# Metaformer block on one core: values stored with zeros between a pair's heads, one gated product and one output matmul a tile

## The chip, the cores and the metric

The kernel runs on one core of one Trainium2 chip, in float32. The metric is the device time of one execution, in microseconds; the median of several runs is compared.

## The reference

The input x is (16, 64, 64, 64): n images, rows a, columns b, 64 channels. Four sublayers follow one another, each added to x; this change touches the first alone, attention over the image axis.

```
zn  = layernorm(z) * ln_w + ln_b                 # over the 64 channels
q,k,v = zn@Wq, zn@Wk, zn@Wv                      # 8 heads of 16 channels
g   = sigmoid(zn @ Wg + bg)
att = softmax over j of q[i,a,b,h,:] . k[j,a,b,h,:] / 4      # i, j: the 16 images
out = (sum_j att[i,j] * v[j]) * g, reshaped @ Wo + bo
```

Then: a router picks 2 of 8 experts (softmax, top 2, renormalized) per token; an exponential moving average over the rows a gates a linear expansion; last, an expert-choice layer for each image (32 experts, 8 tokens each), which is the kernel's second stage.

## The kernel before

**Steps.** The first stage holds the first three sublayers. Its unit is half a column b: 4 tiles (QT) of 128 tokens, a token block being 8 rows a by 16 images. 64 columns of two halves give 128 steps. In the code a step is `step(i, q)`, column i, half q; q = 0 is called an even step here, q = 1 an odd one. The stages of a half are spread over successive steps by the table `LAG` (projections lag 1, scores 2, values and output 3, experts 4, expansion 5, moving average's output 7), so that within one step every engine works on several halves. Each engine has its own program, written out by hand in a fixed order, the same in every step; semaphores alone tie them (`filled[...]`, `drained[...]`, `s_og`, ...). Only even steps hold the moving average: its scan on VectorE (L926) and its tanh `ema_t` on ScalarE (L564). The gating product `gated` (L800) is computed at the end of the even step for one half, and in the midst of the odd step for the other.

**Attention in a step.** TensorE transposes a normalized half; ScalarE copies it to `zT`. Four projections follow: q, values (L670), gate, k (L608 and L609, the last into `s_bank`). ScalarE makes eight masked copies of the keys, `kT`, one a head (L472), spread over its program (heads 0 to 1, 2 to 3, 4 to 5, 6, and 7 as the last of the step). A step later L640 multiplies them with the queries: 32 tokens at a time, two accumulating products each, to give the scores in `s_bank`. VectorE takes the maximum and subtracts it, ScalarE takes exp, VectorE sums and inverts, with `own_den` (L857) made so that each head of a pair gets its denominator or zero. GpSimd multiplies these out into `probs` (L414), which holds for every pair of heads two blocks, one with the first head's probabilities and zeros, one with the second's; VectorE transposes (L918).

**The values.** ScalarE copies the values out of PSUM into `v_sb` (L504); GpSimd adds their bias (L406). L658 multiplies, for each tile t, each pair of heads k and each group g of 32 tokens, the 32 x 32 block of `v_sb` (both heads of the pair) with 64 moving columns of `probsT`. The result `o_bank` has 64 columns a tile and group, 32 for each head of a pair, and in either only one head's rows are meant. VectorE multiplies both halves with the gate `gT` into `ogT` (L839, twice), and L687 multiplies them with the output weights, two accumulating matmuls a tile: `w_o2[:, 0]` keeps the first heads' rows, `w_o2[:, 1]` the second heads' (the factor 0.5 of the sigmoid is in them). The gate is tanh of half its argument (ScalarE, `gT`, L512), plus one (ScalarE, L561, late in the step); the sigmoid is half of that.

**Who waits for whom around it.** `gT` is written when its last reader `ogT` is done (`s_og`). L640 waits for the last key copy (`drained["k"]`). The x1 sum (L868 on VectorE) waits for L687. The router's chain follows on VectorE up to `lgm` (L888), and ScalarE's `lge` (L541) waits for that; the last four key copies stand behind `lge` on ScalarE.

A float32 matmul appears in the trace as two matmul records and two weight loads.

## Time and profile before

| | |
|---|---|
| three timed runs | 3136.28 us median, 3127.79 to 3141.26 |
| profiled execution | its span is 3121.5 us; no other time of it is given |
| TensorE matmul, weight loads | busy 2647.5 us (85%), 1969.9 us (63%) |
| VectorE | busy 2551.6 us (82%) |
| ScalarE | busy 2005.1 us (64%) |
| GpSimd | busy 2161.0 us (69%) |
| mean granted TensorE clock | 0.839 of full |
| L658 value products | 16384 records, 196.5 us |
| L687 output products | 2048 records, 246.9 us |
| L406 add of the values' bias | 128 of 1274 ns on GpSimd |
| L839 `ogT` | 256 of 679 ns on VectorE |

The span is from the first to the last instruction. A busy share is a mean over all stages; the first stage takes nearly all of the span. Matmul records overlap, so the busy time of a group is the time in which at least one of them ran.

### The profile page before, as it was taken

What the parts mean: (1) busy time and instruction counts of PE and PEld (TensorE: products, weight loads), DVE (VectorE), ACT (ScalarE), POOL (GpSimd) and SP (SyncE); (2) the same over time, 40 slices, a digit from 0 to 9 for tenths busy, and PEclk for the clock granted to TensorE, in tenths of its full rate; (3) what the DMA queues carried; (4) which work ended last, traced back from release to release, by engine and by line L of the source; (5) the groups of instructions that cost most, each with busy time, mean ns of one, the idle gap of its engine ahead of it and who ended that gap; (6) DMA issues with size and microseconds to landing.
All of it is one profiled execution on the core that took longest, in us unless ns stands there. A gap on an engine that the chain in (4) does not pass through costs nothing. (4 is left out here: it accounts for less than half of the span.)

```text
span 3121.5 us, 108500 instructions
## 1 busy us (share of the span) xinstructions
PE 2647.5 (85%) x37071; PEld 1969.9 (63%) x37071; DVE 2551.6 (82%) x9002; ACT 2005.1 (64%) x3590; POOL 2161.0 (69%) x2963
## 2 busy tenths in 40 slices
PE   2898898888888888898898898888988988896697
PEld 2666666666666656666666666666666666664586
DVE  2788889888888898888888888888889888885604
ACT  2666767766676676776776766677667676762600
POOL 2677777877777777777787877778777777863000
PEclk9788988887888888888887987889889788885858
DMA  0011101111011010110101111011010010101828
GB/s 17 9 20 18 19 17 19 19 18 19 17 19 18 18 19 17 19 19 18 19 17 18 19 18 19 17 19 19 18 19 18 17 19 18 19 15 19 269 96 337
DMA packets 263153, 106.67 MB, mean 34 GB/s; under 512 B 250257, under 2 KB 254900, under 8 KB 258997
## 3 DMA queue, kind: packets, MB, share of 16 engines
q1 hardware_dynamic: 260933, 93.16, 12.9%
q10 hardware_dynamic: 2160, 12.68, 1.0%
q8 instruction: 40, 0.66, 0.1%
q14 instruction: 20, 0.16, 0.0%
HBM read 55.31 MB, written 50.33 MB: 34 GB/s over the span
## 5 line engine op out<-in xcount | busy, mean ns | idle before, releaser
L472 ACT ACTIVATE kT<-s_bank,b_k,block_of 128x512 f32<-128x512 f32 x1024 | 748.8, 771 | 3.6 <-PE s_bank L609 0.3
L640 PE MATMUL s_bank<-kT,qT 128*32 128x128 f32 x8192 | 396.1, 372 | 187.3 <-issue 187.3
L640 PEld LDWEIGHTS s_bank<-kT,qT 128*32 128x32 f32 x8192 | 349.5, 152 | 226.8 <-issue 224.7
L489 ACT ACTIVATE qT<-shared,b_qkg 128x256 f32<-128x256 f32 x256 | 107.5, 471 | 412.0 <-PE shared L609 412.0
L811 DVE TENSOR_REDUCE mixed<-yg 128x256 f32<-128x2048 f32 x128 | 288.5, 2254 | 0.2
L687 PEld LDWEIGHTS o_bank<-w_o,ogT 128*128 128x128 f32 x2048 | 247.9, 193 | 23.7 <-DVE ogT L839 14.8
L414 POOL TENSOR_TENSOR probs<-weights,own_den 128x1024 f32<-128x1024 f32 x128 | 252.7, 1975 | 1.8 <-DVE own_den L857 1.8
L687 PE MATMUL o_bank<-w_o,ogT 128*128 128x64 f32 x2048 | 246.9, 274 | 4.3 <-DVE ogT L839 3.9
L387 POOL TENSOR_TENSOR split_ffn<-norm_ffn,split_ffn 128x256 fp32r<-128x256 f32 x128 | 93.6, 731 | 215.1 <-ACT split_ffn L464 215.1
L658 PEld LDWEIGHTS o_bank<-probsT,v_sb 32*32 32x32 f32 x16384 | 170.2, 107 | 63.7 <-issue 58.1
L658 PE MATMUL o_bank<-probsT,v_sb 32*32 32x64 f32 x16384 | 196.5, 234 | 1.5 <-DVE yg L932 1.5
L387 POOL TENSOR_TENSOR split_att<-norm_att,split_att 128x256 fp32r<-128x256 f32 x128 | 94.0, 735 | 147.4 <-ACT split_att L464 147.4
L622 PE MATMUL shared<-bias,ones 3*128 3x512 bf16 x256 | 109.3, 427 | 98.3 <-ACT picks L532 52.2
L555 ACT ACTIVATE gpre<-shared,bgate_col 64x256 f32<-64x256 f32 x256 | 181.4, 709 | 13.3 <-PE shared L721 10.3
L593 PE MATMUL shared<-ident,split_att 128*128 128x128 f32 x512 | 111.6, 357 | 69.3 <-ACT prim L555 47.9
L377 POOL TENSOR_TENSOR rstd_ffn<-rstd_ffn,minus_half 128x4 f32<-128x4 f32 x128 | 160.1, 1251 | 10.7
L406 POOL TENSOR_TENSOR v_sb<-v_sb,bv_rows 128x512 f32<-128x512 f32 x128 | 163.1, 1274 | 3.0 <-ACT v_sb L504 3.0
L839 DVE TENSOR_TENSOR ogT<-o_bank,gT 128x512 f32<-128x512 f32 x256 | 163.2, 679 | 1.5 <-PE o_bank L658 1.2
L918 DVE STREAM_TRANSPOSE probsT<-probs 128x1024 f32<-128x1024 f32 x128 | 157.9, 1234 | 2.0 <-POOL probs L414 2.0
L593 PEld LDWEIGHTS shared<-ident,split_att 128*128 128x128 f32 x512 | 78.4, 182 | 123.3 <-issue 68.2
L800 DVE SCALAR_TENSOR_TENSOR gated<-ema_t,prim 64x256 f32<-64x256 f32 x256 | 150.3, 587 | 6.8 <-ACT ema_t L564 1.1
L677 PE MATMUL shared<-w_con,gated 128*128 128x64 f32 x1024 | 141.8, 283 | 7.9 <-DVE gated L800 5.8
(204 smaller groups left out, 7648.6 us busy)
## 6 DMA issues: line engine op xcount, KB each, us to landing
x_in<-in_x SPq DMA_DIRECT2D x1024, 16.0 KB, 1.7
x_scratch<-x SPq DMA_DIRECT2D x1024, 16.0 KB, 1.4
normalized_x_scratch<-norm_pick SPq DMA_DIRECT2D x1024, 16.0 KB, 1.5
xa<-normalized_x_scratch SPq DMA_DIRECT2D x16, 1024.0 KB, 8.1
xb<-x_scratch ACTq DMA_DIRECT2D x8, 1024.0 KB, 10.3
out_x<-xa SPq DMA_DIRECT2D x16, 512.0 KB, 5.3
out_x<-xb SPq DMA_DIRECT2D x16, 512.0 KB, 6.9
xa<-x_scratch SPq DMA_DIRECT2D x4, 1024.0 KB, 6.5
```

The source lines that it names most:

```text
L377: ch.link(g.tensor_tensor(r[:, 1, :], r[:, 0, :], minus_half[:], ALU.pow))
L387: g.tensor_tensor(split[kind][z][:, :, 1, :], norm[kind][z][:], split[kind][z][:, :, 0, :].bitcast(F32), ALU.subtract).then_inc(s_split[ki ...
L406: g.tensor_tensor(v_sb[z][:], v_sb[z][:], bv_rows[:].unsqueeze(1).broadcast_to([P, QT, HC]), ALU.add).then_inc(s_v, 1)
L414: g.tensor_tensor(probs[:], weights[:].unsqueeze(2).broadcast_to([P, 32, 2, 16]), own_den[:].unsqueeze(3).broadcast_to([P, 32, 2, 16]), AL ...
L472: ins = s.activation(kT[:, h, :], bk("k")[:], ACT.Identity, bias=b_k[:, h:h + 1], scale=block_of[:, h:h + 1])
L555: ins = s.activation(dst, src, ACT.Identity, bias=bias[r0:r0 + D], scale=scale)
L593: ins = t_.transpose(bank_of(q, name)[:, t * P:(t + 1) * P], split[kind][par(q, lag)][:, t].rearrange("p k d -> p (k d)").bitcast(F32), id ...
L640: ins = t_.matmul(s_bank[g * 32:(g + 1) * 32, 0, t * P:(t + 1) * P], qT[z][:, c, tok:tok + 32], kT[:, :, tok + c * N:tok + (c + 1) * N], s ...
L658: ins = t_.matmul(o_bank[k * 32:(k + 1) * 32, g, t * 64:(t + 1) * 64], v_sb[z][g * 32:(g + 1) * 32, t, k * 32:(k + 1) * 32], pT[g * 32:(g ...
L687: ins = t_.matmul(bk("att_out")[:, t * D:(t + 1) * D], ogT[:, h, tile(t)], w_o2[:, h, :], start=(h == 0), stop=(h == 1))
L811: v.tensor_reduce(mixed[:], yg[:], AX.X, ALU.add).then_inc(s_mixed, 1)
L839: ins = v.tensor_tensor(by_group(ogT[:, h, :]), o, by_group(gT[z][:]), ALU.mult)
```

## The change

The values are stored with zeros between the heads of a pair: `v_sb` has, for each tile and pair, three slots of 16 channels, and only the outer two are written; the middle one is set to zero once, ahead of the steps. A 32-wide window over slots 0 and 1 is the first head with zeros, one over slots 1 and 2 zeros with the second head. L658 becomes two products for each tile, pair and group, one a head, each with 32 moving columns, added up in PSUM. So `o_bank` has 32 columns a tile and group, all of them meant, and `ogT` becomes one scalar_tensor_tensor: (product + values' bias, now a column) times gate. The output takes one matmul a tile. Since the bias is added there, GpSimd's add to `v_sb` is gone; in its place in GpSimd's program stands gate plus one, and ScalarE's is gone. `zT` and `gT` are written with the order of 32-token blocks exchanged, so that `ogT` reads and writes straight runs. The bias column comes from a fourth matmul of the setup.

```diff
@@ weights and buffers
-            w_o2 = cb("w_o2", [P, 2, D])
+            w_o2 = cb("w_o2", [P, D])
-            bv_rows = cb("bv_rows", [P, HC])
+            bv_col = cb("bv_col", [P, 1])
-            v_sb = cpair("v_sb", [P, QT, HC])
+            v_sb = cpair("v_sb", [P, QT * 4, 3, C])
-            ogT = cb("ogT", [P, 2, QTOK])
+            ogT = cb("ogT", [P, QTOK])
@@ GpSimd
-                        pool.wait_ge(drained["v"], at(i, q, 1))
-                        g.tensor_tensor(v_sb[z][:], v_sb[z][:], bv_rows[:].unsqueeze(1).broadcast_to([P, QT, HC]),
-                                        ALU.add).then_inc(s_v, 1)
+                        wait_apart(pool, (drained["gate"], at(i, q, 1)))
+                        g.tensor_scalar(gT[z][:], gT[z][:], 1.0, None, ALU.add).then_inc(s_gp1, 1)
@@ ScalarE
-                        s.copy(zT[z1][:], bk("att_t")[:]).then_inc(drained["att_t"], 1)
+                        s.copy(zT[z1][:].rearrange("p (g t i) -> p t g i", g=4, t=QT),
+                               bk("att_t")[:].rearrange("p (t g i) -> p t g i", g=4, t=QT)).then_inc(drained["att_t"], 1)
-                        s.copy(v_sb[z1][:].rearrange("p t c -> p (t c)"), bk("v")[:]).then_inc(drained["v"], 1)
+                        s.copy(v_sb[z1][:, :, 0:3:2, :], bk("v")[:].rearrange("p (k m c) -> p k m c", m=2, c=C)).then_inc(drained["v"], 1)
-                        s.activation(gT[z1][:], bk("gate")[:], ACT.Tanh, bias=bg_col[:],
+                        s.activation(gT[z1][:].rearrange("p (g t i) -> p t g i", g=4, t=QT),
+                                     bk("gate")[:].rearrange("p (t g i) -> p t g i", g=4, t=QT), ACT.Tanh, bias=bg_col[:],
-                        act.wait_ge(drained["gate"], at(i, q, 1))
-                        s.activation(gT[z1][:], gT[z1][:], ACT.Identity, bias=one_col[:]).then_inc(s_gp1, 1)
@@ TensorE
-                        wait_apart(pe, (s_probsT, at(i, q, 3)), (s_v, at(i, q, 3)), (s_og, at(i, q, 4)),
+                        wait_apart(pe, (s_probsT, at(i, q, 3)), (drained["v"], at(i, q, 3)), (s_og, at(i, q, 4)),
-                                for g in range(4):
-                                    ins = t_.matmul(o_bank[k * 32:(k + 1) * 32, g, t * 64:(t + 1) * 64],
-                                                    v_sb[z][g * 32:(g + 1) * 32, t, k * 32:(k + 1) * 32],
-                                                    pT[g * 32:(g + 1) * 32, t, 2 * k:2 * k + 2, :],
-                                                    tile_position=(g * 32, k * 32))
+                                for h in range(2):
+                                    for g in range(4):
+                                        rows = slice(g * 32, (g + 1) * 32)
+                                        ins = t_.matmul(o_bank[k * 32:(k + 1) * 32, g, t * 32:(t + 1) * 32],
+                                                        v_sb[z][rows, t * 4 + k, h:h + 2, :].rearrange("p m c -> p (m c)"),
+                                                        pT[rows, t, 2 * k + h, :], start=(h == 0), stop=(h == 1),
+                                                        tile_position=(g * 32, k * 32))
-                            for h in range(2):
-                                ins = t_.matmul(bk("att_out")[:, t * D:(t + 1) * D], ogT[:, h, tile(t)], w_o2[:, h, :],
-                                                start=(h == 0), stop=(h == 1))
+                            ins = t_.matmul(bk("att_out")[:, t * D:(t + 1) * D], ogT[:, tile(t)], w_o2[:])
@@ VectorE
-                        by_group = lambda a: a.rearrange("p (t g i) -> p g t i", g=4, i=32)
-                        for h in range(2):
-                            o = o_bank[:, :, 0:QT * 64].rearrange("p g (t h i) -> p g t h i", h=2, i=32)[:, :, :, h, :]
-                            ins = v.tensor_tensor(by_group(ogT[:, h, :]), o, by_group(gT[z][:]), ALU.mult)
-                        ins.then_inc(s_og, 1)
+                        rows_of = lambda a: a.rearrange("p (g x) -> p g x", g=4)
+                        v.scalar_tensor_tensor(rows_of(ogT[:]), o_bank[:, :, 0:QT * 32], bv_col[:], rows_of(gT[z][:]), ALU.add,
+                                               ALU.mult).then_inc(s_og, 1)
```

Three places show what moves. The first is TensorE's program in a step of the loop, around the value products (L658 before, L650 after), from the end of the scores on; `w_qkg` are the projection weights.

```order
L640 MATMUL s_bank<-kT,qT 32x128 x31
L608 MATMUL shared<-zT,w_qkg_hi 128x512 [waits drained_y3,drained_att_t]
L609 MATMUL shared<-zT,w_qkg_lo 128x512
L658 MATMUL o_bank<-probsT,v_sb 32x64 [waits o_gated,drained_y2,values_biased,drained_route,probs_transposed,pool_setup]
L658 MATMUL o_bank<-probsT,v_sb 32x64 x63
L593 MATMUL shared<-ident,split_ffn 128x128 [waits split_ffn,drained_att_t]
```

And the same place of the changed program:

```order
L630 MATMUL s_bank<-kT,qT 32x128 x31
L598 MATMUL shared<-zT,w_qkg_hi 128x512 [waits drained_y3,drained_att_t]
L599 MATMUL shared<-zT,w_qkg_lo 128x512
L650 MATMUL o_bank<-probsT,v_sb 32x32 [waits o_gated,drained_y2,drained_v,drained_route,probs_transposed,pool_setup]
L650 MATMUL o_bank<-probsT,v_sb 32x32 x127
L583 MATMUL shared<-ident,split_ffn 128x128 [waits split_ffn,drained_att_t]
```

The products doubled in number with half the columns, and their wait for the biased values became one for ScalarE's copy. The second place is ScalarE's program at the end of an odd step, from `lge` to the last key copy (L541 and L472 before, L537 and L466 after).

```order
L541 ACTIVATE lge<-lgm 128x32 [waits top_diff]
L472 ACTIVATE kT<-s_bank,b_k,block_of 128x512 x2
L207 REGISTER_ALU [waits filled_expand]
L555 ACTIVATE gpre<-shared,bgate_col 64x32x8 [waits gated_done]
L555 ACTIVATE prim<-shared,bprim_col 64x256
L555 ACTIVATE gpre<-shared,bgate_col 64x32x8
L555 ACTIVATE prim<-shared,bprim_col 64x256
L472 ACTIVATE kT<-s_bank,b_k,block_of 128x512
L561 ACTIVATE gT<-gT,one_col 128x512 [waits drained_gate]
L472 ACTIVATE kT<-s_bank,b_k,block_of 128x512
```

After:

```order
L537 ACTIVATE lge<-lgm 128x32 [waits top_diff]
L466 ACTIVATE kT<-s_bank,b_k,block_of 128x512 x2
L205 REGISTER_ALU [waits filled_expand]
L551 ACTIVATE gpre<-shared,bgate_col 64x32x8 [waits gated_done]
L551 ACTIVATE prim<-shared,bprim_col 64x256
L551 ACTIVATE gpre<-shared,bgate_col 64x32x8
L551 ACTIVATE prim<-shared,bprim_col 64x256
L466 ACTIVATE kT<-s_bank,b_k,block_of 128x512 x2
```

The second pass over `gT` is gone from between the last two key copies. The third is GpSimd's program around the old add to `v_sb` (L406 before; L402 after).

```order
L257 REGISTER_ALU
L380 TENSOR_TENSOR norm_conv<-norm_conv,rstd_conv 128x256 [waits pool_norm_conv]
L406 TENSOR_TENSOR v_sb<-v_sb,bv_rows 128x512 [waits drained_v]
L387 TENSOR_TENSOR split_conv<-norm_conv,split_conv 128x4x64 [waits rounded_conv]
L207 REGISTER_ALU [waits denominators]
L414 TENSOR_TENSOR probs<-weights,own_den 128x1024 [waits probs_transposed]
```

After:

```order
L255 REGISTER_ALU
L376 TENSOR_TENSOR norm_conv<-norm_conv,rstd_conv 128x256 [waits pool_norm_conv]
L402 TENSOR_SCALAR gT<-gT 128x512 [waits drained_gate,pool_setup]
L383 TENSOR_TENSOR split_conv<-norm_conv,split_conv 128x4x64 [waits rounded_conv]
L205 REGISTER_ALU [waits denominators]
L409 TENSOR_TENSOR probs<-weights,own_den 128x1024 [waits probs_transposed]
```

The instruction at this place now works on `gT`, and waits for the gate's tanh instead of the copy of the values.

## Rows read from the trace of the kernel before

**Rows 1.** The page, first line.

```profile
span 3121.5 us, 108500 instructions
```

**Rows 2.** Waits, 500 to 2500: us in total, times, longest.

```profile
ACT lge L541 <- DVE lgm L888: 89.3, 92, 2.3
...
ACT gT L512 <- DVE ogT L839: 19.4, 22, 1.5
...
DVE x L868 <- PE o_bank L687: 18.5, 46, 0.9
```

**Rows 3.** Timeline, even step: start us, us, engine, line, operation, idle before.

```profile
1515.10 3.42 PE L640 MATMUL s_bank<-kT,qT 128*32 128x128 f32 x64
...
1523.62 0.40 PE L609 MATMUL s_bank<-zT,w_qkg_lo 128*128 128x512 f32 x1
...
1529.44 0.23 ACT L541 ACTIVATE lge<-lgm 128x32 f32<-128x32 f32 x1 [0.44 <-DVE lgm L888]
...
1533.56 1.22 DVE L926 TENSOR_TENSOR_SCAN ema<-decay,gpre 128x512 f32<-128x512 f32 x1
...
1534.82 1.08 ACT L564 ACTIVATE ema_t<-ema 128x512 f32<-128x512 f32 x1
...
1535.80 0.76 ACT L472 ACTIVATE kT<-s_bank,b_k,block_of 128x512 f32<-128x512 f32 x1
...
1536.66 3.64 PE L640 MATMUL s_bank<-kT,qT 128*32 128x128 f32 x64 [2.44 <-issue]
```

**Rows 4.** Timeline, an odd step.

```profile
1451.07 3.64 PE L640 MATMUL s_bank<-kT,qT 128*32 128x128 f32 x64 [2.45 <-issue]
...
1461.71 0.84 DVE L800 SCALAR_TENSOR_TENSOR gated<-ema_t,prim 64x256 f32<-64x256 f32 x2
...
1466.28 0.23 ACT L541 ACTIVATE lge<-lgm 128x32 f32<-128x32 f32 x1 [0.51 <-DVE lgm L888]
...
1472.46 1.95 PE L640 MATMUL s_bank<-kT,qT 128*32 128x128 f32 x64 [1.47 <-issue]
```

**Rows 5.** Timeline, another odd step.

```profile
1622.57 2.61 PE L640 MATMUL s_bank<-kT,qT 128*32 128x128 f32 x64 [0.66 <-issue]
...
1625.77 1.47 PE L658 MATMUL o_bank<-probsT,v_sb 32*32 32x64 f32 x128
...
1630.19 0.39 PE L609 MATMUL s_bank<-zT,w_qkg_lo 128*128 128x512 f32 x1
...
1632.08 2.38 DVE L800 SCALAR_TENSOR_TENSOR gated<-ema_t,prim 64x256 f32<-64x256 f32 x2
...
1632.04 1.27 POOL L406 TENSOR_TENSOR v_sb<-v_sb,bv_rows 128x512 f32<-128x512 f32 x1
...
1637.98 0.23 ACT L541 ACTIVATE lge<-lgm 128x32 f32<-128x32 f32 x1 [2.25 <-DVE lgm L888]
...
1644.11 2.15 PE L640 MATMUL s_bank<-kT,qT 128*32 128x128 f32 x36 [1.00 <-issue]
```

**Rows 6.** L658 on TensorE in 0.5 us: stretch, us, busy (records), clock, DMA.

```profile
1519.75:1520.25 0.50, 0.50 (x76) 1.00 0.00 0
```

**Rows 7.** Costliest groups, whole run: busy us, mean ns, idle before.

```profile
L687 PE MATMUL o_bank<-w_o,ogT 128*128 128x64 f32 x2048 | 246.9, 274 | 4.3 <-DVE ogT L839 3.9
...
L658 PE MATMUL o_bank<-probsT,v_sb 32*32 32x64 f32 x16384 | 196.5, 234 | 1.5 <-DVE yg L932 1.5
...
L839 DVE TENSOR_TENSOR ogT<-o_bank,gT 128x512 f32<-128x512 f32 x256 | 163.2, 679 | 1.5 <-PE o_bank L658 1.2
...
L555 ACT ACTIVATE gpre<-shared,bgate_col 64x256 f32<-64x256 f32 x256 | 181.4, 709 | 13.3 <-PE shared L721 10.3
```

**Rows 8.** Groups of ScalarE by line, whole run.

```profile
L561 ACT ACTIVATE gT<-gT,one_col 128x512 f32<-128x512 f32 x128 | 90.9, 710 | 0.0
```

**Rows 9.** L640 on TensorE in two stretches, columns as in rows 6.

```profile
1451.10:1454.60 3.50, 3.50 (x64) 0.50 0.08 13
1472.50:1474.40 1.90, 1.90 (x64) 1.00 0.18 30
```

More of the change, by code:

```diff
@@ L183, in build @@
             s_top, s_diff, s_ratio, s_gates = sem("top_chain"), sem("top_diff"), sem("top_ratio"), sem("gates_done")
-            s_sums, s_v = sem("exp_summed"), sem("values_biased")
+            s_sums = sem("exp_summed")
             s_mixed, s_x2, s_x2bc = sem("experts_mixed"), sem("x2_done"), sem("x2_bc_done")
@@ L190, in build @@
             N_LOADS = 34
-            N_POOL_SETUP = 12
-            N_DVE_SETUP = 11
+            N_POOL_SETUP = 10
+            N_DVE_SETUP = 10
             def at(i, q, lag, n=1, more=0):
@@ L355, in _ @@
                 setup(g.memset(decay[:, :, 0:1], 0.0))
-                setup(g.memset(one_col[:], 1.0))
                 setup(g.memset(top2[:], NEVER))
-                setup(g.memset(bv_ones[:], 1.0))
                 setup(g.memset(minus_half[:], -0.5))
@@ L447, in _ @@
                     s.mul(w_scaled[:, m, :], w_raw[:, m, :], lnw_col[:]).then_inc(s_act_setup, 1)
-                s.mul(bv_terms[:], w_raw[0:D, 3, :], lnb_col[0:D]).then_inc(s_act_setup, 1)
                 act.wait_ge(s_pe_setup, 7)
                 s.copy(b_qkg[:], shared[1][:, 0:3]).then_inc(s_act_setup, 1)
-                s.copy(bv_rows[:], shared[1][:, P:2 * P]).then_inc(s_act_setup, 1)
+                s.copy(bv_col[:], shared[1][:, 3:4]).then_inc(s_act_setup, 1)
                 s.copy(w_expand_hi[:], shared[0][:, 0:P]).then_inc(s_act_setup, 1)
@@ L455, in _ @@
                 s.copy(w_pick[:], shared[0][0:D, 2 * P:2 * P + EP]).then_inc(s_act_setup, 1)
-                act.wait_ge(s_act_setup, 11)
+                act.wait_ge(s_act_setup, 10)
                 act.wait_ge(s_dve_setup, N_DVE_SETUP)
@@ L580, in _ @@
                 t_.transpose(shared[0][0:D, 2 * P:2 * P + EP], gw_raw[:], ident[0:EP, 0:EP]).then_inc(s_pe_setup, 1)
-                for m in range(3):
+                for m in range(4):
                     t_.matmul(shared[1][:, m:m + 1], w_raw[0:D, m, :], lnb_col[0:D]).then_inc(s_pe_setup, 1)
-                pe.wait_ge(s_act_setup, 6)
-                pe.wait_ge(s_pool_setup, N_POOL_SETUP)
-                t_.matmul(shared[1][:, P:2 * P], bv_ones[:], bv_terms[:]).then_inc(s_pe_setup, 1)
-                pe.wait_ge(s_act_setup, 11)
+                pe.wait_ge(s_act_setup, 10)
                 pe.wait_ge(s_pool_setup, N_POOL_SETUP)
@@ L742, in _ @@
                 dve.wait_ge(s_weights, 16 * N_LOADS)
-                dve.wait_ge(s_act_setup, 11)
+                dve.wait_ge(s_act_setup, 10)
                 v.memset(gated[0][:], 0.0)
                 v.memset(gated[1][:], 0.0)
+                v.memset(v_sb[0][:], 0.0)
+                v.memset(v_sb[1][:], 0.0)
                 v.memset(qT[0][:], 0.0)
@@ L761, in _ @@
                 setup(v.tensor_scalar(bg_col[:], bg_col[:], b_qkg[:, 2:3], 0.5, ALU.add, ALU.mult))
-                for h in range(2):
-                    setup(v.tensor_scalar(w_o2[:, h, :], w_o[:], odd_even[:, h:h + 1], 0.5, ALU.mult, ALU.mult))
+                setup(v.tensor_scalar(w_o2[:], w_o[:], 0.5, None, ALU.mult))
                 setup(v.tensor_tensor(by_channel(bias_rest[:]), bias_row[:].rearrange("o (e c) -> o c e", e=NE),
```

3 lines of the change are left out of this document (removed).

## The prediction

> **What bounds the kernel now.** I read first the page and its fortieths, to see that stage one is all that counts, then the waits of three engines over 2,000 us of its steady part, then the timeline of single steps. The span is 3121.5 us [rows 1]; the median of the three timed runs is 3136.28 us, 14.8 us more, and I add that 14.8 back at the end. The change lies in stage one alone (128 steps; some 93 of them lie in the stretch of the waits, in which `lge` waited 92 times [rows 2]).
>
> A step, counted from the first scores product (L640) to the next one, is a ring. Look at the last key copy of a step, 1535.80 plus 0.76, which ends at 1536.56, and at the scores of the next step, which start at 1536.66 [rows 3]. TensorE had stood idle for 2.44 us. The view calls it "issue", but what it waited for is that copy. So the ring is: TensorE runs without a pause from L640 to the end of the key projection (L609 into s_bank), part A; from there ScalarE works through `gT`, six key copies and what lies between them up to `lge` (L541), part F; then the rest, up to the last key copy, part G. What only makes TensorE shorter behind the key projection shortens no step by itself.
>
> Three kinds of step. An even step (rows of 1515.10): A = 1524.02 - 1515.10 = 8.92, F = 1529.44 - 1524.02 = 5.42, G = 7.22 [rows 3]. An odd step that TensorE leads (1451.07): A + F = 1466.28 - 1451.07 = 15.21, G = 6.18 [rows 4]. An odd step that VectorE leads (1622.57): A = 8.01, F = 7.40, G = 6.13 [rows 5]. In the last, VectorE came late to `ogT`, so that `gT` waited for it, and `lge` waited 2.25 us. `gT` waited for `ogT` 22 times in those 93 steps [rows 2]: I take it that 22 of some 46 odd steps are of this kind, 24 of the other.
>
> **The change, part by part.** *The value products (L658), in part A.* One burst is 128 records now; each of 64 matmuls being two of them; they become those of 128 matmuls with half the moving columns. 76 records were in flight or started in a window of 0.50 us; a record lasts about 0.23 us, so they start 0.50 + 0.23 over 76 = 9.6 ns apart [rows 6, 7]. That is far less than their own length, so many run side by side, and I take them to be bound by how fast they start, not by columns. 128 more records x 9.6 ns = **1.2 us** more in A, in all 128 steps. Bounds: below, 0 (if columns set the pace, their number is unchanged: 64 x 64 = 128 x 32); above, a stop at every second product (rivals). I choose the issue pace because the weight loads, 32 columns each, double too.
>
> The Trainium skill, page "TensorEngine Tiling (Array Packing)", section "Instruction Overhead", speaks against this edit: each matmul carries some 60 cycles, so one of 32 moving columns takes as long as one of 60. At 2.4 GHz that is 25 ns, and by it 128 more records would be an estimated 3.2 us. By that rule the old burst of 128 would have taken 3.2 us, and the row shows 1.47 us [rows 5]; so the trace does not bear it out for products that are spread over the array.
>
> *One output matmul a tile (L687).* 246.9 us in 128 steps is 1.93 a step for 16 records; 8 records take half, 0.96 [rows 7]. It lies behind the key projection, off A. What it gives is what waited for it: VectorE's `x1` add (L868) 18.5 us in 46 waits, 0.40 each [rows 2]. `lge` waits for VectorE in nearly every step, so the 0.40 reaches it, in even steps. I take **-0.40 in even steps**. In odd steps VectorE has `gated` (0.84 us, L800) ahead of L868 and came to it with no wait worth counting [rows 4]: 0.
>
> *One `ogT` on VectorE.* Two instructions of 679 ns [rows 7] become one scalar_tensor_tensor over as many elements as one of them. Bounds 0.68 and 1.36; it reads one operand from PSUM and one from SBUF as the old one does, so I take 0.68, a gain of 0.6 to 0.7. In steps that TensorE leads, VectorE then waits longer for the scan's output: nothing. In steps that VectorE leads, it counts.
>
> *Gate plus one.* ScalarE loses L561, 0.71 us a step [rows 8]. In odd steps it stands directly ahead of the last key copy: **-0.71**, and TensorE had 1.00 and 1.47 us of idle there [rows 4, 5], so it can take it. In even steps `ema_t` follows it, which waits for the scan: 1533.56 + 1.22 = 1534.78, and `ema_t` started at 1534.82 [rows 3]. So there L561 was cover for a wait, and its removal gives at most **0.04**.
> GpSimd loses the add to `v_sb` (1.27 us [rows 5]) and gains a one-operand add over the same count: between half of it and all of it. It now waits for `gT` instead of `v_sb`; behind it on GpSimd stand `split_conv`'s second part, `probs`, `x_bo`. `split_conv` waits for ScalarE's cast, which comes after two key copies (1.44 us) behind `gT`; so up to 1.27 us is covered. If that cover were gone, `probs` would move, and its reader (L918) is far behind.
>
> *Copies into another layout (L480, L504, L512).* Same element counts in runs of 16 or 32. An output whose neighbours lie far apart costs more (`gpre` 709 ns for 256 elements [rows 7]), against 710 for 512 contiguous [rows 8]. Runs of 32 are nearer to contiguous: I take 0; the other end is +0.35 in `gT` alone, the only one on the ring. The setup is under a microsecond either way.
>
> **The sum.** Even: +1.2 - 0.40 - 0.04 = +0.76; I take 0.1 off, since some even steps must be led by VectorE too (my choice): +0.66. Odd, TensorE leads: +1.2 - 0.71 = +0.49. Odd, VectorE leads: TensorE would now put `lge` at 8.01 + 1.2 + 5.42 = 14.63; VectorE had it at 8.01 + 7.40 = 15.41, less 0.6 = 14.8, and less again where the first `gated`, which with its twin took 2.38 us instead of 0.84 while GpSimd's add to `v_sb` ran [rows 4, 5], is no longer held up. I take 14.66, a gain of 0.75, and 0.71 behind it: -1.46. Odd mean: (24 x 0.49 - 22 x 1.46) / 46 = -0.44. A pair of steps +0.22; 64 pairs **+14 us**: a span of 3135.5, a time of 3150 us.
>
> **Rivals.** *(a) The halved columns pay, the pace of starts does not double.* With +0.3 instead of 1.2: even -0.24, odd TensorE-led -0.41; in the VectorE-led, 14.4 or less against 15.41 gives -1.0 and -0.71; odd mean -1.03; pair -1.27, 64 pairs -81; VectorE's own time stops part of it, as it then leads more steps: -40 to -80 us, near 3075. Decides from an added burst time under about 1.0 us, where the pair turns negative. For it: the records overlap heavily. Against: loads double as well.
> *(b) The second product of a pair goes to the same part of the array only four matmuls after the first.* If its load had to sit out the first's 0.23 us, less the 0.07 that the three others fill, 16 such stops would add 2.6 us to the 1.2. Even +3.3, odd +2.5, 64 pairs about +370 us. Against it: the scores do the same (second product after four matmuls, accumulating), and a burst of 64 records took 1.95 us at 2.4 GHz [rows 4, 9], eight rounds at 0.24, no more than their own streaming. A partial stop (+2.0 instead of 1.2) gives +1.6 a pair, about +100 us. That the page's rule holds after all would be +3.2: A grows by 3.2 in every step, +2.7 even, +1.5 odd on average, +270 us; I give it 3 in 100, inside this rival's 12.
> *(c) The clock.* The scores' burst took 3.64 us after 2.45 us of idle, at a granted clock of 0.50, which is 1.2 GHz, and 1.95 us at a clock of 1.00, 2.4 GHz, after 1.47 of idle [rows 4, 9]. The change takes idle from in front of odd steps' ends and puts some behind the shorter output matmuls. If a quarter more of the steps ran their scores slow, 32 x 1.7 = +54 us; a quarter fewer, -54. I can't tell the sign, and it is the widest term.
> *(d) GpSimd's new add holds up VectorE* at `own_den` and `gated` in odd steps that TensorE leads, since it starts later than the old one: +0.5 in 24 of 46 odd steps, +17 us.
>
> **How the numbers follow.** My forecast (the sum, within about 30 us) 0.50; (a) 0.18; (b) 0.12; (c) beyond 30 us on the slow side 0.12, on the fast side 0.08. (d) is inside the forecast's width. A measurement of this kernel tells 0.5%, some 16 us, from no change. The forecast lies just under that on the slow side: of its 0.50, 0.02 is faster, 0.30 within, 0.18 slower. With (a) and the fast clock: faster 0.27, same 0.32, slower 0.41. Range for 8 in 10: from 3080, most of (a), to 3215, most of the slow clock and a small stop of (b).
>
> **What would show it.** In the profile of the changed kernel: the value burst 2.5 to 2.8 us for 256 records; L687's successor 8 records in about 1 us; one `ogT` of 0.68; ScalarE without the second `gT`, and an idle of some 0.6 before `ema_t`; the waits for L868 gone; VectorE's wait for `ogT`'s reader gone from the list of `gT`. Even steps longer by 0.7, odd ones shorter by 0.4. A value burst of under 2.2 or over 3 us, or a mean granted clock over the stage that moves, would make the prediction wrong.

## The result, and the profile after

Three runs: 3214.95 us median (3205.98 to 3215.15), against 3136.28. The ratio is 1.0238, 95% interval 1.0201 to 1.0276: slower, and on the side that had the largest chance, but 65 us above the forecast of 3150 and only 0.05 us inside the upper end of the range, 3215. The profiled execution took 3214.95 us itself, its span is 3213.2, the mean granted clock of TensorE 0.817 (0.839 before).

The page of the kernel after, first line, and then from its costliest groups (busy us, mean ns of one record, idle us before):

```profile
span 3213.2 us, 139089 instructions
...
L630 PE MATMUL s_bank<-kT,qT 128*32 128x128 f32 x8192 | 402.6, 378 | 180.1 <-issue 180.1
...
L650 PE MATMUL o_bank<-probsT,v_sb 32*32 32x32 f32 x32768 | 308.0, 198 | 24.7 <-issue 24.7
...
L402 POOL TENSOR_SCALAR gT<-gT 128x512 f32<-128x512 f32 x128 | 196.9, 1538 | 143.5 <-ACT gT L507 143.4
```

L630 is the scores (L640 before), L650 the value products (L658), L402 GpSimd's gate plus one. The value products have twice the records of before in 1.57 times the busy time [rows 7]; the plus one lasts 1538 ns, where I had allowed 0.64 to 1.27 us.

The groups of the stretch 500 to 2500 us, same columns:

```profile
L678 PE MATMUL o_bank<-w_o,ogT 128*128 128x64 f32 x720 | 89.9, 268 | 0.0
L828 DVE SCALAR_TENSOR_TENSOR ogT<-o_bank,bv_col,gT 128x512 f32<-128x512 f32 x90 | 66.8, 742 | 19.4 <-PE o_bank L650 17.5
L613 PE MATMUL o_bank<-w_expert_hi,tT 128*128 128x512 f32 x91 | 59.0, 649 | 0.0
L876 DVE COPY top<-top 128x8 f32<-128x8 f32 x90 | 50.3, 559 | 3.1
L846 DVE TENSOR_TENSOR own_den<-ssum,odd_even 128x64 f32<-128x64 f32 x90 | 33.9, 377 | 3.1
```

One `ogT` of 742 ns stands for two of 679 [rows 7]. L613, an expert matmul, serves as a gauge of the clock in the middle of a step: it takes 0.50 or 0.51 us at full clock and 0.80 at half (the timelines below), so a mean of 649 ns says that about half of these records ran at half clock. In the kernel before the mean was 581 ns (L623 there).

Waits in the same stretch (us in total, times, longest):

```profile
PE s_bank L630 <- issue: 122.4, 45, 2.7
PE shared L697 <- issue: 46.1, 90, 0.9
...
PE shared L583 <- POOL split_conv L383: 18.9, 23, 0.8
```

```profile
ACT ema_t L557 <- DVE ema L915: 38.3, 45, 0.9
ACT lge L537 <- DVE lgm L877: 36.1, 90, 0.9
```

The `x1` add's wait for the output product and `gT`'s wait for `ogT` [rows 2] are gone from the list, and `lge` waits 0.40 us a step instead of 0.97. Yet the kernel is slower. The first row tells where to look: TensorE waits at the scores in 45 of 90 steps only. In the other half it comes to the scores last itself.

An even step and the odd one behind it, in the timeline (start us, us, idle before):

```profile
1480.52 3.38 PE L630 MATMUL s_bank<-kT,qT 128*32 128x128 f32 x64
...
1484.49 2.35 PE L650 MATMUL o_bank<-probsT,v_sb 32*32 32x32 f32 x256
...
1489.87 0.39 PE L599 MATMUL s_bank<-zT,w_qkg_lo 128*128 128x512 f32 x1
...
1495.01 0.23 ACT L537 ACTIVATE lge<-lgm 128x32 f32<-128x32 f32 x1 [0.24 <-DVE lgm L877]
...
1498.13 0.51 PE L613 MATMUL shared<-w_expert_hi,tT 128*128 128x512 f32 x1
...
1500.63 1.08 ACT L557 ACTIVATE ema_t<-ema 128x512 f32<-128x512 f32 x1 [0.85 <-DVE ema L915]
1501.61 0.76 ACT L466 ACTIVATE kT<-s_bank,b_k,block_of 128x512 f32<-128x512 f32 x1
...
1502.47 1.95 PE L630 MATMUL s_bank<-kT,qT 128*32 128x128 f32 x64 [2.71 <-issue]
...
1510.32 0.39 PE L599 MATMUL s_bank<-zT,w_qkg_lo 128*128 128x512 f32 x1
...
1513.62 0.64 PE L697 MATMUL shared<-lT,w_pick 64*32 64x128 f32 x8 [0.84 <-issue]
...
1515.08 1.09 PE L583 MATMUL shared<-ident,split_conv 128*128 128x128 f32 x4 [0.82 <-POOL split_conv L383]
...
1516.10 0.60 PE L612 MATMUL shared<-bias,ones 3*128 3x512 bf16 x1
...
1521.22 1.45 ACT L466 ACTIVATE kT<-s_bank,b_k,block_of 128x512 f32<-128x512 f32 x2
1522.54 0.80 PE L613 MATMUL shared<-w_expert_hi,tT 128*128 128x512 f32 x1
1523.14 0.63 PE L614 MATMUL shared<-w_expert_lo,tT 128*128 128x512 f32 x1
...
1524.55 0.87 PE L630 MATMUL s_bank<-kT,qT 128*32 128x128 f32 x12
```

In the even step the end is as it was [rows 3]: last key copy, then the scores, TensorE idle for 2.71 us. In the odd step the last key copy is done at 1521.22 + 1.45 = 1522.67, and the scores start at 1524.55 with no idle: TensorE was still at its experts. From L612 at 1516.10 to the end of L614 at 1523.77 these took 7.67 us, at a granted clock of 0.50; in the step behind this one, at 1.00, the same block took 4.48 (1538.59 to 1543.07). The windows say which clock (busy of PE, PEld, DVE, ACT, POOL, then granted clock):

```profile
1502.47:1513.50 11.03, 10.31 (x366) 9.45 (x366) 10.59 (x31) 6.52 (x14) 7.47 (x11) 1.00 0.07 12
1513.50:1524.55 11.05, 10.11 (x31) 4.83 (x31) 8.66 (x42) 7.67 (x14) 9.55 (x13) 0.53 0.13 24
```

The first half of this odd step has 2.4 GHz, the second 1.2 GHz but for its very start. The mean step, counted over all 127 distances between starts of the scores, went from 21.52 to 22.22 us: 127 x 0.70 = 89 of the span's 92 us. Over steps 20 to 119 even ones went from 21.76 to 22.03 us, odd ones from 21.55 to 22.34.

Here are these 100 steps by the prediction's parts, mean us: A from the first scores record to the end of the key projection, F from there to `lge`, G from there to the next scores. "Scores" is the scores' burst inside A, "block" the experts' block measured above. The last two rows belong to the ninth and tenth experiments, which have the old value products.

| | even: A, F, G | scores, block | odd: A, F, G | scores, block |
|---|---|---|---|---|
| before | 8.60, 5.54, 7.61 | 3.07, 5.67 | 8.78, 6.50, 6.27 | 3.02, 5.77 |
| after | 9.82, 4.75, 7.47 | 3.46, 4.45 | 9.38, 5.85, 7.10 | 2.80, 7.42 |
| ninth | 7.46, 5.31, 7.45 | 1.95, 4.45 | 9.74, 5.43, 5.57 | 3.64, 4.45 |
| tenth | 7.54, 5.43, 7.22 | 2.00, 4.50 | 8.67, 5.98, 6.17 | 2.85, 4.45 |

From before to after A grows in both kinds of step and F shrinks in both. Part G shrinks a little in even steps and grows by 0.83 in odd ones, where the experts' block now runs at half clock.

### The profile page after: what moved, and what is told of

It is laid out like the page before. It is cut to its first block and busy times, and to the rows that moved or that the text cites. A ratio compares the mean times of both kernels' runs of the same rounds, so it can differ in the third digit from the quotient of the medians.

```text
span 3213.2 us, 139089 instructions
## 1 busy us (share of the span) xinstructions
PE 2725.6 (85%) x52431; PEld 2021.8 (63%) x52431; DVE 2501.7 (78%) x8875; ACT 1926.8 (60%) x3461; POOL 2192.9 (68%) x2961
## 5 line engine op out<-in xcount | busy, mean ns | idle before, releaser
L466 ACT ACTIVATE kT<-s_bank,b_k,block_of 128x512 f32<-128x512 f32 x1024 | 743.0, 773 | 3.4 <-PE s_bank L599 0.2
L630 PE MATMUL s_bank<-kT,qT 128*32 128x128 f32 x8192 | 402.6, 378 | 180.1 <-issue 180.1
L630 PEld LDWEIGHTS s_bank<-kT,qT 128*32 128x32 f32 x8192 | 348.2, 156 | 228.0 <-issue 215.1
L650 PEld LDWEIGHTS o_bank<-probsT,v_sb 32*32 32x32 f32 x32768 | 292.2, 104 | 81.9 <-issue 81.7
L650 PE MATMUL o_bank<-probsT,v_sb 32*32 32x32 f32 x32768 | 308.0, 198 | 24.7 <-issue 24.7
L402 POOL TENSOR_SCALAR gT<-gT 128x512 f32<-128x512 f32 x128 | 196.9, 1538 | 143.5 <-ACT gT L507 143.4
L494 ACT CAST tT<-shared 128x512 fp32r<-128x512 f32 x128 | 75.0, 586 | 220.2 <-PE shared L583 220.2
L837 DVE TENSOR_TENSOR x<-shared,x_bc 128x256 f32<-128x256 f32 x128 | 54.0, 422 | 181.4 <-PE shared L669 181.4
L613 PE MATMUL shared<-w_expert_hi,tT 128*128 128x512 f32 x256 | 157.4, 615 | 0.0
L612 PE MATMUL shared<-bias,ones 3*128 3x512 bf16 x256 | 119.6, 467 | 44.4 <-ACT picks L528 41.1
L369 POOL TENSOR_TENSOR norm_conv<-x,mv_conv 128x256 f32<-128x256 f32 x128 | 79.1, 618 | 103.3 <-DVE mv_conv L773 103.2
L791 DVE SCALAR_TENSOR_TENSOR gated<-ema_t,prim 64x256 f32<-64x256 f32 x256 | 142.2, 555 | 6.4 <-ACT ema_t L557 1.1
L662 PE MATMUL shared<-w_scaled,zT 128*128 128x128 f32 x1024 | 139.0, 280 | 3.9 <-issue 2.0
```

The lines of the kernel that those rows point to most:

```text
L402: g.tensor_scalar(gT[z][:], gT[z][:], 1.0, None, ALU.add).then_inc(s_gp1, 1)
L466: ins = s.activation(kT[:, h, :], bk("k")[:], ACT.Identity, bias=b_k[:, h:h + 1], scale=block_of[:, h:h + 1])
L613: t_.matmul(bk(y)[:], tT[z4][:, tile(t)], w_expert_hi[:], start=False, stop=False)
L630: ins = t_.matmul(s_bank[g * 32:(g + 1) * 32, 0, t * P:(t + 1) * P], qT[z][:, c, tok:tok + 32], kT[:, :, tok + c * N:tok + (c + 1) * N], s ...
L650: ins = t_.matmul(o_bank[k * 32:(k + 1) * 32, g, t * 32:(t + 1) * 32], v_sb[z][rows, t * 4 + k, h:h + 2, :].rearrange("p m c -> p (m c)"), ...
L791: ins = v.scalar_tensor_tensor(gated[q][rows, :, h * 8:(h + 1) * 8], ema_t[rows, half, :], 1.0, prim[rows, half, :], ALU.add, ALU.mult)
```

## The experiments

The letters in the expectations: C lays the loss to TensorE's pauses and clock, G to GpSimd's new add, V to the doubled value products. Ratios are to the kernel before on the same chip, with their 95% intervals.

**The gate plus one back on ScalarE.**

```diff
 # GpSimd, ahead of split_conv
-g.tensor_scalar(gT[z][:], gT[z][:], 1.0, None, ALU.add).then_inc(s_gp1, 1)
 # ScalarE, ahead of the last key copy
+s.activation(gT[z1][:], gT[z1][:], ACT.Identity, bias=one_col[:]).then_inc(s_gp1, 1)
```

> The changed kernel with gate plus one back on ScalarE, ahead of the last key copy; GpSimd has nothing in that place. Theory G (GpSimd's gate plus one, 1.54 us, holds up its split_conv and with it TensorE): clearly faster than the changed kernel's 3215, 3160 to 3185. Theory C (TensorE idles in mid-step since the output product is shorter, its clock falls, and odd steps end TensorE-bound at half clock): a little faster, 3190 to 3205, as ScalarE's 0.71 us lies in slack. Theory V (the longer value products alone): within 10 us of 3215, or slower by up to 40 where ScalarE sets the end.

1.0231 (1.0181 to 1.0281), as the kernel after: theory G missed. Its median of 3199.34 us lies in C's range, but on this chip the kernel before was 10 us faster too (3125.87), so it does not part C from V. Whether ScalarE or GpSimd adds the one is worth nothing here.

**Twice the output product.** Each tile's output matmul twice, accumulated, the weights halved, so that TensorE works as long there as before.

```diff
-    ins = t_.matmul(bk("att_out")[...], ogT[:, tile(t)], w_o2[:])
+    for h in range(2):
+        ins = t_.matmul(bk("att_out")[...], ogT[:, tile(t)], w_o2[:], start=(h == 0), stop=(h == 1))
```

> The changed kernel with the output product issued twice a tile (weights halved, the two added up in PSUM: the same result), so TensorE has its old 16 records there. Theory C: faster in spite of more work, 3130 to 3185, granted clock up from 0.817 towards 0.84. Theories G and V: the same or slower, 3215 to 3240.

1.0163 (1.0118 to 1.0208), a median of 3179.69 us: not slower than after, perhaps a little faster (the intervals just overlap), in spite of 8 records more a step. Clocks were 0.852 to 0.871. That is what C foretold, and not G or V.

**The gate plus one last in GpSimd's step.** The same instruction, moved behind `x2_bc`.

> The changed kernel with gate plus one still on GpSimd, but as the last instruction of its step, behind split_conv, probs and the normalizations. Theory G: 3160 to 3185 like the ScalarE version, or better. Theory C: 3190 to 3210. Theory V: 3210 to 3220.

1.0077 (1.0048 to 1.0107), 3148.36 us: two thirds of the loss gone, as G's "or better" allows. At this point I blamed GpSimd; the ninth experiment shows that this was too quick.

**The kernel before with one output product a tile.** It leaves out the second heads.

```diff
-    for h in range(2):
-        ins = t_.matmul(bk("att_out")[...], ogT[:, h, tile(t)], w_o2[:, h, :], start=(h == 0), stop=(h == 1))
+    ins = t_.matmul(bk("att_out")[...], ogT[:, 0, tile(t)], w_o2[:, 0, :])
```

> The kernel before with the output product of the first heads alone (leaves out the second heads' share of the attention output): 8 records instead of 16, nothing else changed. Theory C: slower than before, 3150 to 3200, with a lower granted clock. Theories G and V: 3105 to 3136, by the 0.40 us that VectorE waited for it in even steps.

0.9873 (0.9825 to 0.9921), 3084.18 us, at a clock of 0.791. The shorter output product by itself is a gain, larger than G and V had it, although the clock falls; C in its plain form, that it must cost, is refuted.

**Old products, gate plus one late.** The kernel after with the values and their products as before (one of 64 columns a tile, pair and group), two `ogT` (each with the bias), two output matmuls; the plus one last on GpSimd.

```diff
-    for h in range(2):
-        for g in range(4): matmul(o_bank[..., t * 32:(t + 1) * 32], v_sb[z][rows, t * 4 + k, h:h + 2, :], pT[rows, t, 2 * k + h, :])
+    for g in range(4): matmul(o_bank[...] (64 columns), v_sb[z][rows, t, k * 32:(k + 1) * 32], pT[rows, t, 2 * k:2 * k + 2, :])
```

> As e3 (gate plus one last on GpSimd, bias in the scalar_tensor_tensor), but with the value products of before (64 a step with 64 moving columns, values without zeros), two ogT and two accumulating output matmuls a tile. Theory V (what is left of the loss is the doubled products in the part between the scores and the keys, 0.88 us in each of 128 steps, 113 us): 3060 to 3095, below the kernel before, since ScalarE is rid of its 0.71 us in odd steps. If the layout, the bias or the scalar_tensor_tensor were what costs: 3120 to 3150.

0.9863 (0.9833 to 0.9894): faster than both kernels. Against its twin with the new products (1.0077) the new products, with the single `ogT` and the single output matmul that belong to them, cost 2.2%.

**First heads' product only, gate plus one late.** It, too, leaves out the second heads.

```diff
-    for h in range(2):
+    for h in range(1):
```

> As e3, but with the first head's product of each pair alone (leaves out the second heads' attention output): 128 records a step with 32 moving columns. If the pace of starts sets the burst, it lasts 1.3 to 1.5 us in place of 2.35, as long as the old one with twice the columns; the time is then 3148 less 0.88 x 128 = 3035, to 3060. If columns counted, the burst would be near 0.8 us.

0.9801 (0.9763 to 0.9838), with the lowest clock of all the profiled executions, 0.769. The time missed its range: 3078.82 us, where 3035 to 3060 was foreseen. The burst came out at the edge of its own range of 1.3 to 1.5:

```profile
1519.53 1.29 PE L650 MATMUL o_bank<-probsT,v_sb 32*32 32x32 f32 x128
```

128 records of 32 columns take 1.29 us, 128 of 64 columns 1.47 [rows 5], 256 of 32 columns 2.35, all at full clock. At the same number of records, half the columns save 12%. At the same number of columns in all, twice the records take 60% more. So it is mostly the number of records that sets the time, as the prediction had it against rival (a).

**The gate plus one behind `split_conv`.** One place later on GpSimd than in the kernel after, so that `split_conv` is not held up.

> As the changed kernel, but with GpSimd's gate plus one one place later, behind split_conv and ahead of probs. Theory G as I tell it (what hurts is split_conv, and TensorE's transposes behind it, held up by the gate's wait and its 1.54 us): 3140 to 3165, near e3's 3148. If it is its load on GpSimd or on the way to probs: 3185 to 3215.

1.0193 (1.0156 to 1.023), 3208.81 us. So it isn't the held-up `split_conv`. In the timeline of an odd step:

```profile
1521.17 1.49 POOL L404 TENSOR_SCALAR gT<-gT 128x512 f32<-128x512 f32 x1
...
1522.64 1.93 POOL L409 TENSOR_TENSOR probs<-weights,own_den 128x1024 f32<-128x1024 f32 x1
...
1523.29 1.31 DVE L876 COPY top<-top 128x8 f32<-128x8 f32 x1
1524.51 0.18 DVE L877 TENSOR_TENSOR lgm<-lg,top 128x32 f32<-128x32 f32 x1
```

VectorE's copy of 8 columns, in the router's chain that `lge` waits for, lasts 1.31 us here and ends with GpSimd's `probs` (1522.64 + 1.93 = 1524.57). The Trainium skill, page "SBUF — State Buffer", section "Who interferes with whom", has the rule: VectorE's copies can run in a mode that takes the ports shared with GpSimd, and whichever of the two engines issues first keeps them for its whole instruction while the other is blocked. The rows agree: the copy and `probs` end together. In the kernel after, 123 of the 128 copies last over 0.30 us, and every one of them ends 25 to 34 ns after a GpSimd instruction that had begun before it.

**Twice the output product, gate plus one late.**

> As e3, with the output product issued twice a tile, as in e2. If the clock's gain outweighs the work, as e2 seemed to say: 3115 to 3140, with a granted clock of 0.86 or more. If the shorter output product is worth having where GpSimd is out of the way, as e4 says: 3155 to 3190.

1.0225 (1.019 to 1.0259), 3214.73 us, above both ranges and 1.5% above the same kernel with one product. With the plus one in mid-step the doubled product had cost nothing (the second experiment): the same edit has another price beside other edits.

**Old products, the gate plus one where the change put it.** The kernel after, with only the products, `ogT` and the output matmuls as before (the edit of the fifth experiment).

> The kernel after with the old value products (one of 64 columns for each tile, pair and group), two ogT and two output matmuls a tile, and the gate plus one where the change put it, on GpSimd ahead of split_conv and probs. Theory S (the add's place on GpSimd costs by itself, whatever the products are): the kernel with the old products and the add last stood at 0.986, the change's own products with the add in mid-step against last at 1.024 against 1.008, so 1.6% on top of 0.986: 1.002, about 50 us above the version with the add last. Rival (the place costs only when the longer product burst has pushed ScalarE's gT late): 0.990 or less. The product step alone is then 1.024 less this one.

0.9519 (0.9489 to 0.9548), 2984.27 us. Theory S missed by 5%; the rival's 0.990 or less holds, but nobody had foreseen so much. The new products, together with the single `ogT` and the single output matmul, cost 1.0238 / 0.9519 = 7.6%, more than the whole change, and the rest of the change is a gain of 4.8%. Moving the plus one to the end helps with the new products and hurts with the old ones (0.986 against 0.952). Groups of 500 to 2500 us:

```profile
L650 PE MATMUL o_bank<-probsT,v_sb 32*32 32x64 f32 x12544 | 154.4, 238 | 0.0
...
L613 PE MATMUL o_bank<-w_expert_hi,tT 128*128 128x512 f32 x98 | 49.0, 500 | 0.0
L847 DVE TENSOR_TENSOR own_den<-ssum,odd_even 128x64 f32<-128x64 f32 x97 | 31.1, 320 | 3.3
L877 DVE COPY top<-top 128x8 f32<-128x8 f32 x97 | 29.1, 300 | 3.3
```

L613 is at 500 ns: in no step do the experts run at half clock. And TensorE waits at the scores in every step (98 of 98):

```profile
PE s_bank L630 <- issue: 174.6, 98, 2.7
```

**Old products, the gate plus one on ScalarE.** The former with the first experiment's edit: the kernel before, but for the values' bias, which the two `ogT` add, the order of the columns in `zT`, `gT` and `o_bank`, and the value products' wait, which is now for ScalarE's copy.

> The kernel after with the old products, two ogT and two output matmuls, and the gate plus one back on ScalarE: that is the kernel before but for the values' bias, which is added by the two ogT instead of by GpSimd. Theory T (what the change offered was ScalarE's 0.71 us): with it given back, 1.5% above the version with the add late on GpSimd, as with the new products (1.023 against 1.008): 1.001, no different from before. Rival (it was GpSimd's 1.27 us add of the bias that held up VectorE's two-input operations; taking it off is the gain): 0.985 to 0.990, own_den at 0.23 us instead of 0.53.

0.9521 (0.9492 to 0.9551), 2984.06 us; its L613 stands at 501 ns, `own_den` at 225. T missed; the rival was right in direction, with a third at most of what came. So the gain in the change comes with the bias moved into `ogT` and the column order. ScalarE's 0.71 us, taken as a whole, are worth nothing.

The rival's mechanism is real. In the kernel before:

```profile
1524.25 1.27 POOL L406 TENSOR_TENSOR v_sb<-v_sb,bv_rows 128x512 f32<-128x512 f32 x1
1524.69 0.92 DVE L857 TENSOR_TENSOR own_den<-ssum,odd_even 128x64 f32<-128x64 f32 x1
```

`own_den`, with two operands in SBUF, ends 0.09 us after GpSimd's add, at 1525.61. In that kernel 101 of the 128 `own_den` last over 0.30 us. Each of them ends 78 to 85 ns after a GpSimd instruction that had begun before it, 63 after the add and 38 after `norm_conv`. But that is not the whole gain. Groups and waits of 500 to 2500 us, first the kernel before, then the tenth:

```profile
L640 PE MATMUL s_bank<-kT,qT 128*32 128x128 f32 x5900 | 280.6, 368 | 125.1 <-issue 125.0
L857 DVE TENSOR_TENSOR own_den<-ssum,odd_even 128x64 f32<-128x64 f32 x93 | 49.5, 533 | 3.2
```

```profile
L630 PE MATMUL s_bank<-kT,qT 128*32 128x128 f32 x6260 | 238.0, 315 | 188.4 <-issue 188.4
L847 DVE TENSOR_TENSOR own_den<-ssum,odd_even 128x64 f32<-128x64 f32 x98 | 22.0, 225 | 3.4
ACT lge L534 <- DVE lgm L878: 50.9, 97, 1.0
```

`lge` waits 0.52 us a step against 0.97 [rows 2]: 58 us in 128 steps. The scores' burst takes 238.0 / 97.8 = 2.43 us a step against 280.6 / 92.2 = 3.04: 78 us, since it runs at half clock in fewer steps. The two sum to most of the 151 us that came. And the hold of `own_den` does not decide by itself. In the fourth experiment its mean rose to 891 ns and the kernel was 1.3% faster than before. In the first it was 225 ns and the kernel stayed 2.3% slower. The ninth, as fast as the tenth, has an instruction of 1.51 us in GpSimd's place of the bias. What moves the clock of the scores is not shown, nor was the column order ever undone alone.

The table of parts also shows why the plus one looks worthless here. Without it on ScalarE, part G of odd steps is 0.60 us shorter (ninth 5.57, tenth 6.17), near the 0.71 of the prediction. But the scores of all 50 odd steps run at half clock, against some 26 of 50, and take 0.79 us longer (3.64 against 2.85).

**The router's copy off the shared port, in the kernel after.** The copy becomes a tensor_reduce over one element, and `lgm` reads the logits from PSUM, where a second add puts them; the value products, whose bank it is, now wait for `lgm`.

```diff
-    v.tensor_copy(top2[:, :, 0:2], top8[:, :, 0:2])
-    v.tensor_tensor(lgm[:], lg[:], wide(top8[:, :, 0:1]), ALU.subtract)
+    v.tensor_tensor(route, route, rb_all, ALU.add)          # route: the logits' place in PSUM
+    v.tensor_reduce(top2[:, :, 0:2], top8[:, :, 0:2].unsqueeze(3), AX.X, ALU.max)
+    v.tensor_tensor(lgm[:], route, wide(top8[:, :, 0:1]), ALU.subtract)
```

> The kernel after, in which the router's short copy (8 columns, VectorE) becomes a tensor_reduce over one element, and lgm reads the logits from PSUM, where a second add of 0.15 us puts them; so neither reads two operands from SBUF nor is a copy. Theory P (in this kernel GpSimd's probs, pushed late, holds the copy up: 559 ns mean for 8 columns, up to 1.31 us in one step, and lge waits for it): copy and lgm together about 0.35 us, lge's wait gone in part, 0.2 to 0.3 us a step, 25 to 40 us: ratio 1.012 to 1.016. Rival (the hold only moves to the next two-operand instruction, or lge's start isn't what the end of the step hangs on): within 0.4% of after's 1.024.

0.9833 (0.9801 to 0.9866): both theories missed. Its seven runs lay far apart, 3025.52 to 3097.53 us, at clocks from 0.889 down to 0.845, so the size of the gain is uncertain and the interval too narrow. All of them beat the kernel before (3122.03 at best). The profile is of the fastest:

```profile
L613 PE MATMUL o_bank<-w_expert_hi,tT 128*128 128x512 f32 x97 | 54.3, 560 | 0.0
...
L878 DVE TENSOR_REDUCE top<-top 128x8 f32<-128x8 f32 x98 | 15.9, 162 | 3.4
```

0.40 us a step taken from one small copy (559 to 162 ns) is 51 us at most. The kernel after would take 1.0238 x 3135 = 3210 us on this chip, so 112 to 184 us came. The rest goes with the clock, experts at 560 instead of 649 ns; why the clock moved is not shown.

**The same two edits in the version with old products and the late plus one.**

> The fastest version so far that computes everything (old products, gate plus one last on GpSimd, 0.986) with the same two edits to the router's chain. Theory P: its copy takes 418 ns, up to 0.25 of it a hold; 128 steps x 0.2 = 26 us less, 0.978. Rival: TensorE ends the steps there and the ratio stays at 0.986.

0.9887 (0.9859 to 0.9916): the rival held, nothing gained. This version and the fifth experiment have another trouble, single even steps of 25.6 us. In one of the fifth, TensorE's timeline shows:

```profile
1552.52 1.10 PE L667 MATMUL shared<-w_con,gated 128*128 128x64 f32 x8 [1.35 <-ACT tT L494]
...
1554.48 3.51 PE L677 MATMUL o_bank<-w_o,ogT 128*128 128x64 f32 x16
```

`tT` came late, and the output product took 3.51 us instead of 1.89. The windows say what stretched it (columns as in the windows above; the third number from the end is the clock):

```profile
1552.50:1554.40 1.90, 1.88 (x12) 1.75 (x13) 0.73 (x3) 1.13 (x3) 1.73 (x4) 0.99 0.00 0
1554.48:1558.00 3.52, 3.52 (x19) 3.48 (x18) 0.95 (x3) 2.01 (x4) 2.21 (x4) 0.50 0.17 28
```

The granted clock was 0.50 there, and 0.99 just before. Why it fell stays open.

## Why the prediction came out as it did

**The ring, parts A, F and G.** The picture of a step held in all even steps, before and after, and in every step of the two fastest versions. It failed in after's odd steps, and this is the step of the prediction that was wrong: I had let ScalarE's last key copy end them, on the strength of 1.00 and 1.47 us of idle on TensorE [rows 4, 5]. There TensorE ends all 50 of them, with its experts at half clock. Part G of odd steps grew by 0.83 us where -0.71 was foreseen. Even steps grew by 0.27 us instead of 0.7; odd ones grew by 0.79 instead of shrinking by 0.4.

**Value products, +1.2 us.** Right mechanism, too large: 2.35 - 1.47 = +0.88 a step at full clock, 113 us in 128 steps. The pace of starts is 2.35 us over 256 = 9.2 ns a record, not 9.6, and the old burst was not wholly bound by it: 1.47 over 128 is 11.5. In that the columns had a small part. A partial stop of rival (b) would have added 2.0; the row refutes it. (By the prediction's own working the full stop gives odd steps +2.1, not +2.5, and some 350 us in all; nothing hangs on it.) Rival (a) put its turning point at 1.0 us of added burst. The added burst stayed under it, and still the kernel got slower: the turning point was wrong, since the gain in G of odd steps that it was weighed against did not come.

The rule of the Trainium skill, page "TensorEngine Tiling (Array Packing)", section "Instruction Overhead", gave an estimate of 3.2 us more, with 60 cycles for each record. That is nearly four times the 0.88 that came, and counted for each float32 matmul of two records, 1.6 us, it is still nearly twice. The trace doesn't agree with the rule here.

**One output matmul a tile, -0.40 in even steps.** 8 records take 1.00 us, as foreseen, and the wait of the `x1` add is gone. But what lies behind on TensorE, L697, now waits 0.39 us in an even step and 0.84 in an odd one for ScalarE's `lT`, and that wait was not in my sum. By itself the edit gave 1.3% in the kernel before and 1.5% beside the late plus one. In the kernel after it gave nothing.

**One `ogT`, a gain of 0.6 to 0.7.** 742 ns instead of 680: off by 0.06. `gT`'s wait for it is gone from the list of waits. In all, part F shrank by 0.79 us in even steps and 0.65 in odd ones: in even steps that is more than the 0.40 that I had.

**Gate plus one, -0.71 in odd steps.** This term failed. With the new products and with the old, ScalarE or GpSimd makes no difference to the time (1.023 and 1.024; 0.952 and 0.952). In after's odd steps ScalarE is 1.88 us early (1522.67 against 1524.55), in the other kind of them 1.18 (its last key copies start at 1477.89 and take 1.45, the scores start at 1480.52): it is not what is waited for. With the old products G did get 0.60 shorter and the scores' clock took it back. In even steps `ema_t` waits 0.85 in its place, where some 0.6 was predicted. GpSimd's new instruction, 1.54 us, is also longer than my upper bound of 1.27, the length of a two-operand add over the same count; one operand less is not less time there. In the odd step shown `split_conv` starts only when it ends, and TensorE waits 0.82 us for that; the seventh experiment says that this is not the cost. Rival (d), a hold-up of `own_den` beyond the old one, did not come: its mean fell from 533 to 377 ns.

**The values' bias.** I priced GpSimd's lost add only as something that had stretched `gated` in VectorE-led steps. The tenth experiment prices the whole edit, with the column order: 3135.25 - 2984.06 = 151 us, the largest gain in this study. My forecast left most of it out. It came out within 65 us of the result only because most of the loss with the products was left out too, and that is luck.

**The clock, rival (c).** Named as the widest term, and rightly, but looked for in the wrong place: I priced scores run at half clock, 1.7 us each, 54 us for a quarter of the steps. Between before and after the scores' burst hardly moved, 3.05 to 3.13 us on average. What moved was the clock in mid-step, where the experts' 7.67 - 4.48 = 3.19 us are at stake.

Set after against the ninth experiment, which differs in the products and in the number of `ogT` and output matmuls: +1.77 us a step (22.22 less 20.45, counted as above). The longer burst is 0.87 of it. TensorE's lateness in odd steps is 0.72 more: the mean of 1.88 and 1.18 us, less the 0.10 by which the scores follow a copy in any case, over two. At full clock the experts' block would be 3.19 us shorter, and there would be no lateness. Together that is 1.59 of 1.77. That much is read from rows; the last part is not assigned.

What is shown: in the kernel after the experts of every odd step run at half clock, wholly or for the greater part, and with the old products in place no step's do. Of the 100 steps 20 to 119 it was 28 in the kernel before, 50 in after, 0 in the ninth version, 1 in the tenth (steps in which the granted clock falls 9 to 17.5 us behind the scores' start). What is only argued: why it falls there. In after's odd step two pauses of 0.84 and 0.82 us stand ahead of it, but the second experiment, without the first of them, still has 27 such steps of 100, the kernel before has 28 with neither in its list of waits, and the sixth version, with the shortest burst, has 80 and is fast. A rule for when it falls doesn't come out of these runs.

**Range and chances.** The range held, at its very edge. Its upper end came from a slow clock, and that is what happened, so the width was right for about the right reason; that it held by 0.05 us is luck. The forecast within 30 us, given a chance of 0.50, failed, and the slow side of (c), given 0.12, is what came. The forecast itself was the sum of two large omissions. By its own last sign the prediction was wrong: the mean granted clock over 500 to 2500 us moved from 0.85 to 0.83. The value burst, 2.35 us, lay below the 2.5 to 2.8 foreseen, but not outside 2.2 to 3.

## What to carry to other kernels

Split a change into its parts before judging it: here one part of the change is worth -4.8% and the other +7.6%. The version that adds the bias in `ogT` and leaves the products alone runs in 2984 us. When two engines end a step in turn, the effects of single edits do not add: the shorter output product was worth -1.5%, nothing and -1.3% beside three sets of other edits, the late add -1.6% and +3.6% beside two. Where TensorE doesn't end the step now, ask how late it would be with its longest block at half clock. And when an edit that shortens one part changes no time, look whether another part ran at a lower clock.

## What the hardware showed

- At full clock, matmuls of 32 x 32 spread over the array start 9.2 to 11.5 ns apart per record (two records for a float32 matmul), with little difference between 32 and 64 columns: 1.29 us for 128 records of 32, 1.47 for 128 of 64, 2.35 for 256 of 32.
- GpSimd's add of a constant to 128 x 512 float32 takes 1.49 to 1.54 us on average, its add of two tensors of that size 1.27.
- VectorE's copy of 8 columns takes 300 to 765 ns on average as a copy, by version of the kernel, and 162 ns as a reduce. The longest copy took 1.92 us (seventh experiment); long ones end with a GpSimd instruction. `own_den`, with two operands in SBUF, ranges from 225 to 891 ns on average; in the kernel before, its long ones end with GpSimd's add of the bias or `norm_conv`. In the kernel after, beside GpSimd's add of a constant, none of its 92 that last over 0.30 us (0.62 at most) ends so: it is stretched there, not held to the end.
- A scalar_tensor_tensor with one operand in PSUM takes 742 ns for 512 elements, the tensor_tensor 679.
- This loop can lock into a pattern: the kernel after repeats a group of four steps of 22.0, 22.1, 22.1 and 22.6 us, the clock falling at the same places; the ninth version repeats one of two steps, 20.2 and 20.7.
- The same output product of 16 records took 1.89 us in one step and 3.51 in another of the fifth experiment, at a granted clock of 0.50.
